# Between two mixtures of experts: the groups' steps in a new order on three engines, and twelve answer tiles moved behind the second experts

## What is computed

```python
x = x + tanh(g_xattn[0]) * attention(_layernorm(x), ctx, ...)
x = x + tanh(g_ffn[0]) * first_experts(_layernorm(x), ...)     # 32 experts, 4 chosen, + shared part of width 704
x = x + tanh(g_xattn[1]) * _wkv(time_decay, time_first, _layernorm(x), ctx)
x = x + tanh(g_ffn[1]) * second_experts(_layernorm(x), ...)    # 8 experts, 2 chosen, + shared part of width 352
# shared part: sh = silu(x @ sw_gate) * (x @ sw_up) @ sw_down
# _wkv, without its scaling by maxima:
#   y_t = (sum_k_v + exp(u + k_t) * v_t) / (sum_k + exp(u + k_t));  sums decay by exp(-exp(time_decay)) per step
```

## Time and profile before

| | us |
|---|---|
| median of 3 runs | 1262.88 (1262.86 to 1263.87) |
| the profiled execution | 1260.7 |
| its span | 1259.0 |
| TensorE busy | 1090.3 |
| VectorE busy | 970.0 |
| ScalarE busy | 871.5 |
| GpSimd busy | 701.5 |

### The profile page before, as it was taken

The page is one execution under the profiler, slowest core; times in us unless marked ns, Lnnn a source line. Parts: engine busy times, 40 slices in busy tenths (PEclk is TensorE's granted clock), DMA queues, the critical chain, the costliest instruction groups (busy, mean ns, idle before and its releaser), DMA issues.

```text
span 1259.0 us, 24057 instructions
## 1 busy us (share of the span) xinstructions
PE 1090.3 (87%) x8360; PEld 631.4 (50%) x8360; DVE 970.0 (77%) x1781; ACT 871.5 (69%) x1516; POOL 701.5 (56%) x610
## 2 busy tenths in 40 slices
PE   6958888888988889888898878799998798889994
PEld 4623344444444444444444466367744354556773
DVE  5999899999999999999999867524333778743334
ACT  3658899999999999999999944235514536333441
POOL 3015988877888787887878842766501004352431
PEclk9979999999999999999999987899999988789997
DMA  6686777889888988898666636659361005013326
GB/s 178 114 155 118 157 162 158 166 165 190 155 168 165 175 180 164 163 169 169 115 111 114 109 66 189 191 158 277 115 235 71 1 20 153 35 69 104 96 93 212
DMA packets 388191, 176.36 MB, mean 140 GB/s; under 512 B 329805, under 2 KB 373042, under 8 KB 388072
## 3 DMA queue, kind: packets, MB, share of 16 engines
q1 hardware_dynamic: 381368, 157.84, 57.6%
q0 software_dynamic: 6480, 16.77, 4.0%
q10 hardware_dynamic: 224, 0.20, 0.1%
HBM read 52.70 MB, written 43.59 MB: 76 GB/s over the span
## 4 chain that ended last, share of the span: by engine, by line
PE 50%; DVE 37%; issue 4%; ACT 4%; POOL 2%; DMA 1%; SPq 1%; DVEq 0%; ACTq 0%; POOLq 0%
DVE top L369 23%; PE bank L232 9%; PE bank L218 9%; PE bank L2397 4%; PE bank L250 3%; PE bank L1508 3%; PE bank L1099 3%; PE bank L2413 3%; PE bank L1082 2%; PE bank L1086 2%; PE bank L1525 2%; ACT weight L412 2%; PE bank L1762 2%; DVE x_sb L2090 2%; PE bank L268 1%
## 5 line engine op out<-in xcount | busy, mean ns | idle before, releaser
L412 ACT ACTIVATE weight<-bank,bias,sq_all 128x1024 uint8<-128x1024 f32 x512 | 609.9, 1200 | 33.8 <-PE bank L232 29.1
L369 DVE TENSOR_REDUCE top<-bank 128x1 f32<-128x512 f32 (+1 forms) x683 | 611.1, 952 | 17.0 <-PE bank L218 6.0
L464 POOL CAST weight<-turned 128x2048 bf16<-128x2048 uint8 x256 | 478.8, 1892 | 44.3 <-PE bank L250 25.6
L232 PE MATMUL bank<-kT,query 128*128 128x512 bf16 x1024 | 310.1, 385 | 12.1 <-ACT weight L412 5.2
L250 PEld LDWEIGHTS bank<-v_sb,weight 128*128 128x128 bf16 x4096 | 172.1, 97 | 110.3 <-POOL weight L464 8.2
L218 PE MATMUL bank<-kT,qspace 64*128 64x512 bf16 x687 | 138.2, 395 | 61.4 <-DVE top L369 61.4
L250 PE MATMUL bank<-v_sb,weight 128*128 128x16 bf16 x4096 | 172.8, 170 | 6.7 <-POOL weight L464 6.7
L218 PE MATMUL bank<-kT,query 128*128 128x512 bf16 x337 | 129.6, 385 | 1.6 <-DVE top L369 1.4
L232 PEld LDWEIGHTS bank<-kT,query 128*128 128x128 bf16 x1024 | 60.2, 97 | 104.9 <-ACT weight L412 61.7
L1727 POOL DMA_INDIRECT dispatched_rows<-qspace,put x32 | 39.7, 1239 | 124.3 <-DVE qspace L2192 115.8
L412 ACT ACTIVATION_READ_ACCUMULATOR weight<-bank,bias,sq_all 128x1 f32 x512 | 101.6, 198 | 0.0
(11 more groups left out here) (316 smaller groups left out, 1497.2 us busy)
## 6 DMA issues: line engine op xcount, KB each, us to landing
dispatched_rows<-zeros SPq DMA_DIRECT2D x32, 524.0 KB, 3.2
answered_rows<-zeros SPq DMA_DIRECT2D x16, 512.0 KB, 3.1
late<-answered_rows SPq DMA_DIRECT2D x16, 512.0 KB, 5.5
erow<-dispatched_rows SPq DMA_DIRECT2D x39, 131.0 KB
wgu<-in_L_ffn_w_gate SPq DMA_DIRECT2D x26, 176.0 KB
wgu<-in_L_ffn_w_up SPq DMA_DIRECT2D x26, 176.0 KB
wdn<-in_L_ffn_w_down SPq DMA_DIRECT2D x26, 176.0 KB
query<-qspace SPq DMA_DIRECT2D x32, 128.0 KB, 3.1
```

The source lines that it names most:

```text
L232: mm = pe.matmul(unit[u % 2][:, v * 512:(v + 1) * 512], query2[:, t % 2, h, :], kT[:, h // 2, first + v * 512:first + (v + 1) * 512], star ...
L369: ve.tensor_reduce(top[:, first:first + count], bank[:, first % 3:first % 3 + count, :], AX.X, ALU.max).then_inc(s_max, 1)
L412: ac.activation(weight8[:, n % BYTES, u * 1024:(u + 1) * 1024], unit[u], ACT.Exp, bias=bias[:, n:n + 1], scale=sq_all[:, n:n + 1], accum_o ...
L464: po.tensor_copy(weight[:, n % 3, :, :, :].rearrange("p c q two -> p (c q two)"), turned8[:, n % 3, :, :].rearrange("p c q -> p (c q)").bi ...
```

## The change

Six parts.

1. The decays. The bounds on `u_first` and `decay` and the two exponentials of `decay` move from the head of the stretch into the front stage and the attention's end (VectorE before `copy_outputs(0)`, ScalarE behind `exponentials(0)` and `residuals(1)`).
2. The functions are cut finer: a gate and an up product are issued apart (`shared_gate_tensor`, `shared_up_tensor`), `combine` no longer takes the statistics (`first_statistics`, `second_statistics` are steps of their own), each second answer is one step with its bank named.
3. The lists of the three engines are written in a new order. A group's steps now begin right after its combine, between the shared chunks of other groups, and groups follow each other. `combine(2)` and `combine(3)` stand in the first shared group's time. Nearly every silu now stands alone between two table loads.
4. A second buffer `inv_odd` for the inverses, so that `inverse(g)` waits for quotients(g-2) and not for quotients(g-1). `sum_keys(g)` now waits for denominators(g-1), which stands ahead of it on the same engine.
5. The first shared product of the stretch waits for `rows_scaled` (banks 0 and 1) and no longer for ScalarE's last `answers_weighted`, which the first answer (banks 6 and 7) waits for instead.
6. Only group 0's second answers stay in the stretch. Group 0's and then group 1's hidden rows go to `hT_early`, groups 2 and 3 keep the two halves of `hT`. The twelve answers of groups 1 to 3 follow the last block of the second experts, in banks 0 to 5 in turn. VectorE adds group 1's ahead of the final adds, group 2's and group 3's each ahead of the final adds of their own group.

```diff
@@ head of the stretch, TensorE
-                        pe.wait_ge(sx_["answers_weighted"], E0)
-                        for c in range(NW0):
-                            hidden0(1, c)
-                        for k in range(G):
-                            answers0(1, k)
+                        pe.wait_ge(sx_["rows_scaled"], E0)
+                        shared_gate_tensor(pe, 1, 1, 0)
...
+                        shared_gate_tensor(pe, 2, 2, 0)
                         pe.wait_ge(sx_["answers_weighted"], E0)
+                        shared_answers_tensor(pe, 1, 1, 0, 1)
@@ head of the stretch, ScalarE
-                        ac.wait_ge(mx_["decays_bounded"], 1)
-                        ac.activation(decay[:], decay[:], ACT.Exp).then_inc(mx_["decay_steps"], 1)
-                        ac.wait_ge(mx_["decay_steps"], 1)
-                        ac.activation(decay[:], decay[:], ACT.Exp, scale=-1.0).then_inc(mx_["decay_steps"], 1)
                         ac.wait_ge(mx_["decay_steps"], 2)
@@ inverse
-                            if g > 0:
-                                ac.wait_ge(mx_["mixed_ready"], g)
+                            if g >= 2:
+                                ac.wait_ge(mx_["mixed_ready"], g - 1)
@@ where the hidden rows of the second shared part lie
-                    def hidden_at(g, c):
-                        return c + (NW1 if g == NG - 1 else 0)
+                    def second_hidden_rows(g, c):
+                        if g < 2:
+                            return hT_early[:, c, :]
+                        return hT[:, c + (NW1 if g == 2 else 0), :]
@@ combine
-                        def combine(g):
-                            if g >= 2:
-                                ve.wait_ge(sm_["shared_answers_added"], (g + 1) * G)
+                        def combine(g, answers):
+                            ve.wait_ge(sm_["shared_answers_added"], answers)
@@ behind the last block, TensorE
                         pe.wait_ge(sx_["rows_scaled"], E0 + NB1)
-                        second_answers_tensor(pe, NG - 1, 0, G, first_bank=0)
+                        pe.wait_ge(sx_["hidden"], E0 + NB1)
+                        pe.wait_ge(sx_["hidden_copied"], E0 + NB1)
+                        for g in range(1, NG):
+                            for k in range(G):
+                                n = (NG + g) * G + k
+                                if n >= (NG + 1) * G + 6:
+                                    pe.wait_ge(sm_["shared_answers_added"], n - 5)
+                                second_answers_tensor(pe, g, k, last_answers(g, k))
@@ behind the last block, VectorE
-                        second_answers_vector(ve, NG - 1, 0, G, first_bank=0)
-                        ve.wait_ge(sm_["shared_answers_added"], 2 * NG * G)
+                        for k in range(G):
+                            second_answers_vector(ve, 1, k, last_answers(1, k))
                         for g in range(NG):
+                            if g >= 2:
+                                for k in range(G):
+                                    second_answers_vector(ve, g, k, last_answers(g, k))
+                            ve.wait_ge(sm_["shared_answers_added"], (NG + max(g, 1) + 1) * G)
                             ve.wait_ge(s_got[g], 32 * G)
```

511 lines of the change are left out of this document (307 added, 204 removed).

## The result

The changed kernel takes **1231.15 us** (median; 1229.25 to 1234.93), beside 1262.87 of the kernel before in the same session: a ratio of **0.9751, 95% interval 0.9727 to 0.9775**. The prediction was 1232, with a range of 1219 to 1252 and 0.91 on faster. The profiled execution took 1229.25, its span is 1227.5.

The account below looks back on a forecast made before the run. TensorE's queue sets the end: its 226.5 us stretch is 174.1 work, 31.5 idling, 20.9 slowness. Stretch end -34.5, tail +3.4 and front stage +0.4 sum to -30.7: 1230.0 profiled, 1232 median, range 1219 to 1252.

Parts of the forecast that it names:

- the start: First shared product between the expert loops: at 909.9 instead of 910.53, with 0.4 us added in the front stage.
- the gaps: TensorE's idling between the expert loops: 19.2 us against 31.5 before, plus 0.9 for the last hT.
- the slowness: TensorE's lost time between the expert loops: 20.9 us before; forecast 6.8 for low-clock episodes plus 2.0 for twenty restarts.
- walk: Hand-made step-by-step timing of three engine queues from 909.9, ending the stretch at 1095.7 without clock effects.
- The clock: TensorE between the expert loops: two lower-clock episodes, 6.8 us together, bounds 0 and 17; granted clock near 0.93.
- rival (a): No low-clock episode between the expert loops; TensorE stays at 2.4 GHz: 1225 us, chance 0.22.
- rival (d): A drain at each ScalarE table switch puts 8 us on the stretch's path: 1240 us, chance 0.03.
- Dispatch: Rows for the second experts there by 1094.1, TensorE at 1095.7: hidden with 1.6 us to spare.
- Rival (e): Second experts wait for something outside the stretch, such as dispatch or weights; its end stays: 1262 us, chance 0.04.
- The tail: VectorE's final adds after the second experts: eight moved adds at 0.42 cost 3.4 us, bounds 3 to 8.
- Rivals (b): Waits between the expert loops only move; moved answers and start alone count: -7.2, 1256 us, halfway 1244; chance 0.19.
- (c): TensorE falls to 1.2 GHz at the 2.1 us gap and stays there: 1300 us, slower, chance 0.05.

Follow-up runs that it names:

- experiment 3: Changed kernel with the eight second answers of groups 1 and 2 put back between the last chunks of the stretch: 1237.06 us, ratio 0.9782.
- experiment 12: Changed kernel with small GpSimd writes between dispatch scatters and three of group 2's answers added before group 0's final adds: 1215.87 us beside 1256.11, ratio 0.9679.
- experiment 5: The kernel before, run again unaltered: 1264.11 us against 1265.45.
- experiment 2: Changed kernel with the decays' two bounds and two exponentials moved back to the head of the stretch: 1231.51 us, ratio 0.9724.
- Experiment 4: The kernel before with 67 unused products filling ten TensorE waits after 1000: 1258.56 us, ratio 0.9944.
- experiments 6: Changed kernel with the last 12 of GpSimd's 21 gathers held until VectorE has added the four shared answers: 1236.26 us, ratio 0.9767.
- 7: Changed kernel with a small GpSimd write between the eight dispatch scatters of each of groups 0 to 2: 1230.27 us, ratio 0.9725.
- 9: Changed kernel with GpSimd's 21 gathers issued as 11, then 5 after the shared answers, then five singles ahead of experts' scatters: 1230.66 us, ratio 0.9726.
- 10: The kernel before with its 21 gathers issued as 11, then 5 after the shared answers, then five singles: 1265.69 us, ratio 0.9993.
- 11: Changed kernel with gathers paced 11, 5 and five singles, and dispatch scatters of groups 1 and 2 cut into four and four: 1234.04 us, ratio 0.9747.

## Why the prediction was right, and where it was not

**Direction and size: right.** The new order takes idling from TensorE, whose queue sets the end. Work -10.4 holds (experiment 3: eight answers are worth 8.4 to 11.2 in the stretch). The end of the stretch came where it was forecast, 1102.52 for 1102.5. That is luck: against the forecast the start is 5.9 late, the gaps are 4.7 less and the slowness is 1.2 less, and the three cancel. In experiment 12, without late signals, the stretch takes 182.1 for the 192.6 forecast, although 3.70 of that is a wait for rows.

**The start: 909.9 forecast, 915.79 measured.** The step before it took the earlier trace rows's 910.53 as given. It belongs to an execution without the late signal ahead of the first experts; experiment 5 has 917.15 for the same kernel. The part's own price was about right: the first product waits for nothing and the second chunk no longer for silu (experiment 2: 0.79). The 0.4 that the sum has for the front stage is shown by no run: the start of the four shared answers there varies by more, 812.84 to 814.10 in the changed kernel.

**The gaps: 19.2 + 0.9 forecast, 15.4 measured,** of which 4.48 is the late signal. The walk's own gaps are thus 10.9 for 20.1: over by 9. The sample that the prediction gave is the clearest case. It let TensorE wait 2.1 us from 1017.2 for the silu of gate(0,0), put behind denominators(2), inverse(2) and a load, at 1019.3. Allow 5.9 for the later start, and those three are right within 1 us (denominators(2) end at 1020.12, inverse(2) at 1022.31, the load at 1023.60). But ScalarE's order has silu(0,0) ahead of them, at 1016.89, and TensorE's next gate follows its two answers at 1022.55 without a gap. The walk had taken one silu for the next. Some gaps were there at their size: 1.70 for 1.6 behind copy_places(1), 0.80 for 1.1 behind quotients(3), 0.85 for the last hT. Others came at half: the first half has 3.6 us of gaps (84.20 - 80.65) for 7.0, among them 0.85 for 1.6 (the last up product of the first chunk row) and 0.71 for 1.5 behind quotients(0).

**The clock: two episodes forecast, one came;** slowness 7.6 for 8.8 (6.8 + 2.0). The size came out by luck. The episode stands behind the late signal and not behind the 2.1 gap, which never came; it cost 2.4 (5.07 from 1072.12 to 1077.19, for a turning at 0.93 and a half at 1.72) where an episode was priced at 3.4, and the other 5.2 of slowness was 2.0 in the forecast. The granted clock is 0.98, where the prediction named 0.93; two episodes of 8 us at the lower level in 192.6 would by its own terms have been 0.96. In experiment 12, without late signals, it is 1.00, the state that rival (a) named. Experiment 4 shows that idling brings the lower level at one place (3.78 against 1.99) and that it comes at two others behind gaps under 0.7 only; and that taking 21 us of it away returns 3.8 in the stretch. The weakest step is the addition of idling and slowness as if each lay on the path.

**Table loads:** 28 in the stretch, as forecast, and 0.01 to 0.04 us to the next function wherever ScalarE waits for nothing else, so rival (d) is out. The Trainium skill, page "ScalarE: Activation LUTs", section "What ACT_TABLE_LOAD costs", adds a drain to each load; this trace does not agree.

**Dispatch: hidden, by less than I said.** The last scatter's issue ends at 1096.33. In experiment 12 the first rows were used 4.83 after that point (1085.37 to 1090.20), so here they were ready at about 1101.2, an estimate, and TensorE came at 1102.52 for hT. Spare 1.3 for 1.6, though both ends are 7 us later than in the walk. Rival (e) named the right next bound: experiment 12 reaches it.

**The tail: 3.4 forecast, 3.1 measured** (121.98 against 118.90), eight adds in 2 x 1.65. Its lower bound of 3 was close to the value. The wait of 0.58 for fetched answers was not foreseen.

**Rivals (b) and (c)** did not come. Slower would have needed a clock that stays low; its longest time at the lower level after is at 1072 to 1077.

**What is open.** What makes a signal late, and whether it would be late in an execution that is not recorded. Shown: it stands in 12 of 14 traces, of both kernels; it ends with GpSimd's row of indirect DMAs within 0 to 2.7 us in the plain versions; it moves when the row is moved or cut (experiments 6, 7, 9, 10, 11); its total hardly falls by that. Not shown: that the row is enough, for in two traces the same rows of 21 do nothing (the first of the kernel before, and experiment 12). These two differ from the twelve others in one more thing: they hold 17,046 and 17,065 records of semaphore updates, the others 15,289 to 15,429. So where a signal is late, a tenth of the updates is missing from the trace as well, and "remote" may stand just for such a missing record. The recording itself is thus a rival for the cause, as is the chip; no run tested either. Nor could it be told from the traces whether TensorE itself stands still or only its signal is held back, since the profile models the ends of products.

## What to carry to other kernels

When several groups pass through the same three engines, write the order so that each engine's next step was released two steps ago, and check a hand-made walk against the other engine's list item by item: one silu read in the wrong place cost this prediction 2 us in a single gap. Idling and lower clock of the same engine are not two sums to be added: fill the waits and see what comes back before counting the clock as a gain. Take the profile of the kernel before twice, since one execution can lack a delay of 7 us that the next one has, and compare how complete the two recordings are.

## What was not expected of the hardware

- Engines that wait for a product of TensorE and are released 4 to 8 us after its end in the profile, while GpSimd issues indirect DMAs back to back (0.97 to 1.00 each, 0.30 between), in 12 of 14 traces: 10.10 us of idling where 2.50 is usual. The cause is open, the recording included.
- The lower clock without long idling: 4.54 and 5.49 us for a pair of answers that takes 2.83, behind single gaps of 0.27.
- A session, on another chip, in which the unchanged kernel takes 1256.1 where it took 1265.9: 0.8%, four times what the prediction took for the least difference that can be told from none.
